# A graph network's edge loop: nine instead of eight blocks per pair of turns fetched by TensorE, and a reordered prologue

## The reference

```python
def _gatv2_layer(x, src, dst, Wl, Wr, a, b):
    xl = (x @ Wl).reshape(N, H, O)
    xr = (x @ Wr).reshape(N, H, O)
    s = jax.nn.leaky_relu(xl[src] + xr[dst], NEG_SLOPE)
    e = jnp.einsum('eho,ho->eh', s, a)
    m = jax.ops.segment_max(e, dst, num_segments=N)
    ex = jnp.exp(e - m[dst])
    denom = jax.ops.segment_sum(ex, dst, num_segments=N)
    alpha = ex / (denom[dst] + 1e-16)
    out = jax.ops.segment_sum(xl[src] * alpha[:, :, None], dst, num_segments=N)
    return out.reshape(N, H * O) + b
# GIN: agg = segment_sum(relu(x[src] + edge_attr @ W_edge.T + b_edge), dst), then linear, batch norm, relu, linear
```

## Time and profile before

| what | value |
|---|---|
| time, median of 3 runs | 6675.94 us (6675.53 to 6676.13) |
| the profiled execution | 6672.46 us, span of its core 6670.6 us |
| busy: PE, PEld, DVE, ACT, POOL | 82%, 66%, 74%, 69%, 73% |
| DMA | 1096.16 MB, 164 GB/s over the span |

### The profile page before, as it was taken

How to read it: one execution, slowest core, us unless ns; L and a number is a source line. 1 busy time by engine, 2 the same in 40 slices (tenths; PEclk the granted TensorE clock), 3 DMA queues, 4 the chain that set the end, 5 groups by cost and what they waited for, 6 DMA issues and landing times.

```text
span 6670.6 us, 91041 instructions
## 1 busy us (share of the span) xinstructions
PE 5440.5 (82%) x23034; PEld 4434.7 (66%) x23034; DVE 4960.0 (74%) x7160; ACT 4603.5 (69%) x6121; POOL 4896.3 (73%) x5107
## 2 busy tenths in 40 slices
PE   2588888888668888888848888888875999999996
PEld 1476777777457777777736777777764777777774
DVE  7599999999659888888847888888885444333333
ACT  1487877877458888888827888888873555555553
POOL 3777777777677777777767777777767777777774
PEclk9999999999779999999959999999997999999997
DMA  9466666666435555555524555555542444444441
GB/s 377 174 218 216 217 219 217 218 217 215 131 117 163 162 162 163 165 164 166 164 75 147 166 165 165 165 163 162 162 152 82 132 132 136 134 132 132 132 134 57
DMA packets 420529, 1096.16 MB, mean 164 GB/s; under 512 B 162288, under 2 KB 183424, under 8 KB 416278
## 3 DMA queue, kind: packets, MB, share of 16 engines
q1 hardware_dynamic: 242306, 863.40, 35.7%
q0 software_dynamic: 164080, 181.10, 13.0%
q10 hardware_dynamic: 14116, 51.39, 2.0%
HBM read 710.56 MB, written 384.88 MB: 164 GB/s over the span
## 4 chain that ended last, share of the span: by engine, by line
POOL 47%; issue 26%; DVE 14%; ACT 7%; DMA 2%; PE 2%; ACTq 1%; DVEq 0%; POOLq 0%; SPq 0%
POOL sb_xl L512 42%; DVE pG L1137 4%; ACT sb_turn_out L705 3%; POOL sb_hot_f L512 3%; DVE sb_s_run L1179 3%; ACT sb_hot L705 3%; POOL marks L516 2%; DVE sb_s L1412 2%; DMA sb_xl<-xl_table,sb_idx 1%; PE pG L593 1%; DVE sb_mark L1083 1%; DVE sb_e_in L1201 1%; DVE sb_lr L1199 1%; DVE sb_s L1197 1%; ACT pB L705 1%
## 5 line engine op out<-in xcount | busy, mean ns | idle before, releaser
L593 PE MATMUL pG<-sb_xl_parts,sb_hot 128*128 128x476 f32 (+1 forms) x21952 | 5059.9, 389 | 860.4 <-ACT sb_xl L705 618.0
L512 POOL DMA_INDIRECT sb_xl<-xl_table,sb_idx x4704 | 4502.7, 957 | 1450.0 <-issue 1429.0
L593 PEld LDWEIGHTS pG<-sb_xl_parts,sb_hot 128*128 128x128 f32 x21952 | 4222.5, 195 | 1740.5 <-issue 1180.0
L1137 DVE COPY_PREDICATED pG<-sb_pick_turn,pG 128x408 f32<-128x408 int32 (+5 forms) x2352 | 1008.9, 431 | 932.4 <-ACT sb_pick_turn L705 809.2
L705 ACT ACTIVATE sb_hot<-sb_wide 128x1792 fp32r<-128x1792 bf16 x784 | 1316.8, 1693 | 76.7 <-ACT sb_turn_out L705 71.4
L1179 DVE TENSOR_TENSOR_SCAN sb_s_run<-pB,sb_v_in 128x272 f32<-128x272 f32 (+2 forms) x1075 | 1084.4, 1017 | 25.2 <-ACT sb_turn_out L705 4.0
L705 ACT ACTIVATE sb_turn_out<-sb_s_run 128x1088 f32<-128x1088 f32 (+3 forms) x395 | 833.5, 2110 | 10.5 <-DVE sb_s_run L1179 10.3
L705 ACT ACTIVATE sb_xl<-pG 128x136 f32<-128x136 f32 (+3 forms) x826 | 241.2, 294 | 711.2 <-DVE pG L1137 589.5
L1176 DVE TENSOR_TENSOR_SCAN pB<-sb_same_c,pB 128x1024 f32<-128x1024 f32 x294 | 672.1, 2286 | 0.1
L705 ACT ACTIVATE sb_v_in<-sb_v_g 128x1024 f32<-128x1024 f32 x291 | 597.1, 2052 | 0.0
L705 ACT ACTIVATE pB<-sb_mark 128x960 f32<-128x960 f32 x294 | 551.8, 1877 | 11.8 <-DMA sb_mark<-marks 1.4
(11 more groups left out here) (235 smaller groups left out, 2372.8 us busy)
## 6 DMA issues: line engine op xcount, KB each, us to landing
sb_wide<-hots SPq DMA_DIRECT2D x294, 896.0 KB
state_rows<-sb_turn_out SPq DMA_DIRECT2D x294, 576.0 KB
sb_mark<-marks SPq DMA_DIRECT2D x294, 512.0 KB
sb_wide<-codes SPq DMA_DIRECT2D x98, 896.0 KB
hots<-sb_wide SPq DMA_DIRECT2D x98, 896.0 KB, 3.7
sb_xl<-xl_table,sb_idx POOLq DMA_INDIRECT x4704
marks<-sb_hot_f SPq DMA_DIRECT2D x32, 1568.0 KB
agg_rows<-sb_turn_out ACTq DMA_DIRECT2D x98, 512.0 KB
```

What stands on the lines that cost most here:

```text
L512: return pool.indirect_dma_start(out=dst, out_offset=None, in_=table, in_offset=bass.IndirectOffsetOnAxis(ap=index, axis=0))
L593: product = pe.matmul(pG[:, a, 0:GB * n], hot[k][:, m, a * P:(a + 1) * P], rows[:, :, 0:n], start=(m == 0 and part == 0), stop=(m == GB - ...
L1137: return dve.copy_predicated(rows[:, :, 0:n], over(pick_turn[:, k, stage, lo:hi], n), rows[:, :, at:at + n])
```

## The change

It does five things.

1. In the three attention layers the second turn of each pair fetches five blocks by TensorE and eleven by GpSimd; the first stays at four and twelve. The extra block makes the first share of that turn three blocks. `pG` grows from four to five PSUM banks, `pB` shrinks from four to three. The GIN layer keeps four and twelve.
2. To fit, the factor tile `f` in PSUM shrinks from 9 to 5 outputs of 4 heads (612 to 340 values), and the sum scans become four of 20, 16, 16 and 16 channels.
3. ACT computes `neg_h` as Identity with scale and bias from `same`; the tile `neg` and its DVE instruction go.
4. At the start of a layer the first turn's widening, products, selection and copy no longer stand behind `xr_first`.
5. Prologue: the fill is issued after 14 loads, in one loop; six loads of late weights and `w_blk` go behind it; the splitters' round trip moves to ACT's queue; the ranks are shifted by one matmul and a DVE copy.

```diff
+FETCHED = (4, 5)
+PAIR = sum(FETCHED)
+MOST = max(FETCHED)
+SHARES = tuple(((0, n - 2), (n - 2, n)) for n in FETCHED)
+SHARE_BANK = (0, MOST - 2)
+GD = tuple(G - n for n in FETCHED)
+FO = 5
+SUMS = (0, FO * 4, 36, 52, 68)
...
-        pG = ctx.enter_context(nc.psum_tensor("pG", [P, 4, 512], F32))
+        pG = ctx.enter_context(nc.psum_tensor("pG", [P, MOST, 512], F32))
...
             sp.dma_start(pe_src_r, t["src_pe_edges"]).then_inc(s_src, 16)
+            sp.wait_ge(s_zero, 1)
+            with sp.Fori(0, J * C // (B * C)) as i:
+                sp.dma_start(marks_runs[:, bass.ds(i * (B * C), B * C)], zeros[:, 0:B * C]).then_inc(s_filled, 16)
+            sp.dma_start(b_all[:, :], t["b_rows"].partition_broadcast(P)).then_inc(s_late, 16)
...
-            sp.wait_ge(s_rank, 1)
-            sp.dma_start(ranks[1:1 + NB].rearrange("(p b) -> p b", p=P), ranks_i[:, 0, :]).then_inc(s_rank_out, 16)
-            sp.wait_ge(s_rank_out, 32)
-            sp.dma_start(ranks_i[:, 1, :], ranks[0:NB].rearrange("(p b) -> p b", p=P)).then_inc(s_rank_in, 16)
...
+            def code_row(turn, k):
+                sp.dma_start(staged_code[k].rearrange("p (m e) -> p m e", m=GB),
+                             codes[bass.ds(turn, 1), :].rearrange("a (m e) -> (a m) e", m=GB)[:, ECX - EC[k]:ECX].partition_broadcast(P)
+                             ).then_inc(s_code[k], 16)
...
-                        turn_gathers(l * PAIRS + i, k, range(GD))
+                        turn_gathers(l * PAIRS + i, k, range(GD[k]))
...
+                    pe.wait_ge(s_rank, 1)
+                    pe.matmul(pB[:, 512:513], next_lane[:, :], ranks_f[:, 0, B - 1:B], start=True, stop=True).then_inc(s_rank, 1)
...
+            act.dma_start(splitters.rearrange("(p k) -> p k", p=P), split_s[:, :]).then_inc(s_split_out, 16)
+            act.wait_ge(s_split_out, 16)
+            act.dma_start(split_all, splitters.partition_broadcast(P)).then_inc(s_split_in, 16)
...
-                copy(neg_h[:, :, :], neg[:, bass.ds(turn, 1), :].to_broadcast([P, H, G1])).then_inc(s_e_carried, 1)
+                act.activation(neg_h[:, :, :], same[:, bass.ds(turn, 1), :].to_broadcast([P, H, G1]), ACT.Identity, bias=neg_col[:, 0:1], scale=-NEG).then_inc(s_e_carried, 1)
...
-                return act.activation(f_half[:, :, :, 1:G1], wf_arg[:, 1].unsqueeze(1).to_broadcast([P, HALF, H, G]), ACT.Exp)
+                return act.activation(f_part[:, :, :, 1:G1], wf_arg[:, 1].unsqueeze(1).to_broadcast([P, FO, H, G]), ACT.Exp)
...
-                act.wait_ge(s_start, l + 1)
...
                     rows_copied(l * TURNS + 1, l * PAIRS, q, 0)
+                act.wait_ge(s_start, l + 1)
+                act.sem_inc(s_passed, 1)
+                turn_marks((l * PAIRS + 1) * 16, 0)
...
+                for q in range(2):
+                    select_rows(l * TURNS + 1, l * TURNS + 1, l * (2 * TURNS) + q, 0, q)
                 dve.wait_ge(s_xr_first, (l + 1) * 16)
...
-                    scan_sums(f_flat, 0, HALF * H)
+                    scan_sums(f_flat, SUMS[0], SUMS[1])
                     select_stage(1 - k, 1, 1).then_inc(s_pick, 1)
                     dve.wait_ge(s_pick, picks + 4)
-                    scan_sums(f_flat, HALF * H, HALF * H + third)
+                    scan_sums(f_flat, SUMS[1], SUMS[2])
                     select_stage(1 - k, 1, 2).then_inc(s_sel[1], 1)
-                    scan_sums(f_flat, HALF * H + third, V).then_inc(s_sums, 1)
+                    scan_sums(f_flat, SUMS[2], SUMS[3])
+                    scan_sums(f_flat, SUMS[3], SUMS[4]).then_inc(s_sums, 1)
```

More of the change, by code:

```diff
@@ L52 @@
 GROUPS = B // GB
-EC = GE * P
-HOT = GB * EC
+EC = tuple(n * P for n in FETCHED)
+HOT = tuple(GB * n for n in EC)
+ECX, HOTX = max(EC), max(HOT)
 PARTS = 2
@@ L58 @@
 HO = O + 1
-HALF = HO // 2 + 1
+FO = 5
+SUMS = (0, FO * 4, 36, 52, 68)
+LIN_SUMS = (0, 22, 43, 64)
 V = H * HO
@@ L126, in build @@
         at = PARTS * B * TW
[L127 to L130, removed]
+        staged, staged_code = [], []
+        for k in range(2):
+            codes_k = wide[:, at:at + HOT[k] // 2]
+            staged.append(codes_k.bitcast(BF16).rearrange("p (m e) -> p m e", m=GB))
+            staged_code.append(codes_k.bitcast(I16))
+            at += HOT[k] // 2
         left = wide[:, at:at + GB * TW]
@@ L420, in load_code @@
                 sp.sem_inc(s_passed, 1)
-                sp.dma_start(staged_code[k], codes[bass.ds(turn, 1), :].rearrange("a e -> (a e)").partition_broadcast(P)
-                             ).then_inc(s_code[k], 16)
+                code_row(turn, k)
             def tables_out(l):
@@ L562, in _, with share @@
                     gather(node_rows[:, b, 0:C], agg_rows, last_edge[:, b:b + 1]).then_inc(s_nrow[g], 16)
+        def share(k, q, n=TW):
+            shares, banks = (LIN_SHARES, LIN_SHARE_BANK) if n == C else (SHARES, SHARE_BANK)
+            lo, hi = shares[k][q]
+            return lo, hi, banks[q]
         def place(psum, i):
@@ L588, in pe_gather @@
                     pe.sem_inc(s_passed, 1)
-                for a in range(*SHARES[q]):
+                lo, hi, bank = share(k, q, n)
+                for a in range(lo, hi):
                     for m in range(GB):
@@ L592, in pe_gather @@
                             rows = xl_part[part][:, m * GB * TW:(m + 1) * GB * TW].rearrange("p (b c) -> p b c", b=GB)
-                            product = pe.matmul(pG[:, a, 0:GB * n], hot[k][:, m, a * P:(a + 1) * P], rows[:, :, 0:n],
+                            product = pe.matmul(pG[:, bank + a - lo, 0:GB * n], hot[k][:, m, a * P:(a + 1) * P], rows[:, :, 0:n],
                                                 start=(m == 0 and part == 0), stop=(m == GB - 1 and part == PARTS - 1))
@@ L630, in attention_layer @@
                     for k in range(2):
-                        for q in range(len(SHARES)):
+                        for q in range(2):
                             pe.wait_ge(s_wide[q], l * TURNS + 2 * i + (k + 1))
@@ L743, in widen, with widen_both @@
                 act.sem_inc(s_passed, 1)
-                lo, hi = SHARES[q]
+                lo, hi, bank = share(k, q, n)
                 copy(hot[k][:, :, lo * P:hi * P], staged[k][:, :, lo * P:hi * P]).then_inc(s_wide[q], 1)
-            def widen_both(ready, filled, used, k):
-                for q in range(len(SHARES)):
-                    widen(ready, filled, used, k, q)
+            def widen_both(ready, filled, used, k, n=TW):
+                for q in range(2):
+                    widen(ready, filled, used, k, q, n)
             def widen_first(l, i, k, fresh):
@@ L923, in linear_turn @@
                 act.wait_ge(s_sums, turn_all)
-                copy(same_half.rearrange("p (c g) -> p c g", g=G1), same[:, bass.ds(turn, 1), :].to_broadcast([P, C // 2, G1]))
+                copy(same_part.rearrange("p (c g) -> p c g", g=G1), same[:, bass.ds(turn, 1), :].to_broadcast([P, LIN_SUMS[1], G1]))
                 copy(v_lin[:, :, 0:1], lin_run[:, :, G:G1]).then_inc(s_same, 1)
@@ L1193, in attention_turn @@
                 dve.wait_ge(s_xr, turn_all + 1)
-                for q in range(len(SHARES)):
+                for q in range(2):
                     dve.wait_ge(s_rows[q], turn_all + 1)
-                dve.wait_ge(s_xl[k], (use + 1) * (16 * GD))
+                dve.wait_ge(s_xl[k], (use + 1) * (16 * GD[k]))
                 tt(s[:], xl[:, k, :, 0:C], xr.rearrange("p c g -> p g c"), ALU.add).then_inc(s_added, 1)
@@ L1267, in attention_layer @@
                 scan_xr(l * TURNS)
-                for q in range(len(SHARES)):
-                    select_rows(l * TURNS + 1, l * TURNS + 1, l * (2 * TURNS) + q, 0, q)
                 if build:
```

189 lines of the change are left out of this document (92 added, 97 removed).

## The result

The changed kernel takes 6513.83 us (median of 4 runs, 6513.23 to 6514.41), the kernel before 6675.81 (6675.53 to 6676.13). The ratio is 0.9759, 95% interval 0.9746 to 0.9771: 2.4% faster. The profiled executions lie 158.05 us apart (6672.46 and 6514.41), the medians 162.0. Predicted were 155.3 between the profiled executions, and a median of 6521 us in a range of 6502 to 6590. Two slow executions are left out of all ratios: one of the run with a gather left out (14054 us) and one of the kernel before beside the last four runs (9217 us).

A forecast was written before the change was run, and what follows sets the result against it. GpSimd issuing gathers was taken as the bound. Layers two and three 124.4, first layer 21 and prologue 9.9 us sum to 155.3, from 6672.46 to 6517.2 profiled, 6521 us as median; range 6502 to 6590.

The forecast's parts named there:

- The extra block in layers two and three: Second and third attention layers: 23 gathers per pair instead of 24, GpSimd still the bound, each layer saving 61.3 us.
- The scan in four pieces, the wider copies: DVE in layers two and three: copies +0.43 and scans +0.14 us per pair, making its pair 28.51 us.
- TensorE: Attention layers: 126 products take 27.96 us per pair, under GpSimd's 28.78, leaving 0.8 us; clock stays at its upper level.
- The rival at 6590: TensorE takes over in layers two and three: a remaining clock drop makes its pair 29.5 us, +69 us; chance 0.16.
- ACT: Attention turns: widening at most +0.85 us per pair, smaller factor copy saves some; 25.3 of 28.8 us, hidden by idle time.
- the slower rival: ACT reloads tables each turn for Identity in `neg_h`, two loads of 1283 ns; 6800 us; chance 0.07 with anything else slower.
- GpSimd's waits at the layers' start: Layers two and three: waits of 2.39 and 1.25 us for the first turn go, where 0.30 is usual; +3.0 us gained.
- First layer: First attention layer: DVE becomes the bound at 30.78 us per pair, 14 us gained, plus 7 from the earlier start; 21 together.
- Prologue: Before the layers: no ranks' round trip and an earlier fill let the scatters start 9.9 us earlier.
- GIN layer: Layer after the attention layers: claimed not changed in what sets its pace; no term in the sum.

The follow-up runs named there:

- the last four runs: Changed kernel with five blocks in each pair's first turn instead of its second, with and without the late first turn, each twice; ratios 0.977, 0.9775, 0.9785, 0.9788.
- the dose of eight products: Changed kernel with four more TensorE products, sums overwritten, at the start of each attention turn's first share, eight per pair; ratio 0.9907, scaled 6613.7 us.

## Why the prediction was right

- **The extra block in layers two and three**: 61.3 us each by gathers, measured 58.6 with the late start (1616.82 before, 1558.25 with the first turn late). Right. In the third layer it is 58.1. GpSimd stayed the bound by 0.36 us per pair, where 28.78 less 28.51 had given 0.27; DVE's pair is 28.36.
- **The scan in four pieces, the wider copies**: the copy of 612 values took 0.80 us, the 340-value scan 0.865. DVE's pair of 28.51 was 0.15 too long.
- **TensorE**: 27.96 us per pair and 0.8 of slack; the dose of eight products measured 27.94 and 0.78. The share of 42 products took 9.32 us and 98 in a row 21.82, no 7.46 us is left among the steady shares of layers two and three, and the clock is 1.00 there (0.98 in the first layer, where TensorE still waits up to 2.4 us). The rival at 6590 needed one of the clock's drops to stay. The idle time that stood ahead of the slow share, 2.69 us in the earlier trace rows, is gone there: the longest wait is 0.7.
- **ACT**: the widening of 2688 values took 2.44 us (at most 2.54 was allowed), the factor copy 0.42 instead of 0.64. The copy for `neg_h` with scale and bias is 0.34 us, and there are still three table loads in the whole trace, of 1283 ns each. So the slower rival had no base. (Its price was summed a little high as well: 32.4 less 31.07 is 1.33 us, not 1.4.) The Trainium skill ("ScalarE: Activation LUTs", "Table sets: the hidden batching unit") says that cheap functions such as identity are in every table set. The trace agrees: an Identity between exponentials brought no load.
- **GpSimd's waits at the layers' start**: +3.0 us over both layers, but the early start is worth 6.0 + 5.5 in the changed kernel. This is the term that was sized wrong. I took only the waits that the kernel before showed and called them gone. That the extra block itself would lengthen them, by the gather less and by the larger share in front of the multiplication, I did not see. It did no harm, since the change moves the first turn too. With eight blocks the same early start returns nothing (1616.79 us against 1616.82).
- **First layer**: 14 us from the pair and 7 from the earlier start, 21 together; measured 18.7 and 4.6, 23.3. From the first turn's start to the last's, DVE's pair came out at (1727.42 - 5.3 - 239.48) / 48.5 = 30.57 us instead of 30.78. But the kernel before took 30.95 by the same marks, not the 31.07 of the window, so that two errors of 0.21 and 0.12 in part cancel: 0.38 per pair instead of 0.29. GpSimd's pair was put at 29.77 by keeping the mean of a gather; the long gathers come with the builds, two per pair whatever the number of gathers, and the run with a gather left out gives 30.15. That changed nothing, since DVE's is longer. The start gave less because the twelve gathers didn't land 2.3 us after their issue: the first went out at 219.81, the turn began 19.7 us later instead of 17.3. The DMA engines, nearly idle when the first turn began before the change (0.14 between 245 and 253), were full, with loads of codes and a store of one-hot matrices among the work:

```profile
225.00:234.00 9.00, 0.00 (x0) 0.00 (x0) 2.59 (x2) 1.33 (x3) 6.87 (x8) 0.50 0.88 321
234.00:240.00 6.00, 0.00 (x0) 0.00 (x0) 1.67 (x2) 2.37 (x2) 4.78 (x5) 0.50 0.95 366
```

  That this held up the landings is read from these rows, and no run tested it.

- **Prologue**: 9.9 us, measured 9.55. The experiments show that it rests on both edits. The end of the fill near 157, read from the DMA share, was not the end of the wait for it: with the fill late and the ranks known early the scatter went out at 160.03.
- **GIN layer**: called unchanged; it took 2.4 us longer (160.8 to 158.4). The run with eight blocks shows the same layer time within 0.6 us, so it isn't the ninth block's. The GIN layer has edits of its own, which the prediction passed over: with the smaller `pB` its sums are scanned in three pieces (357, 357 and 374 values) where the kernel before has two of 544. No run puts them back, and the cause stays open.

Sum of the measured terms: 9.4 + 23.3 + 64.6 + 63.6 - 2.4 = 158.5, against 158.05 between the profiled executions and 9.9 + 21 + 124.4 = 155.3 predicted. That the sum is only 3 us off is partly luck: layers two and three gave 3.8 us more than said and the first 2.3, and the GIN layer took 2.4 back. The forecast of the median missed by 7 us, of which 4.1 are the offset: it was put 3.5 us above the profiled execution, as before, and lies 0.6 below.

## What to carry to other kernels

When the bound engine issues equal things back to back, one of them less is worth its full period only up to the second engine's distance; find that by a pair's busy and wait time, not by the busy share of the span. A step that costs nothing in the steady state can still cost at the start of every loop, where the lead between engines isn't built up yet: count which buffer the bound engine needs first and what stands in front of the instruction that frees it. Two edits that each shorten a different road to the same start are to be made together: here each alone gave 3.5 or 4.4 us, both 9.55.

## What the runs showed of the hardware

- TensorE's clock at a layer's start. After the products of the first turn it stands still until the second turn's may begin, at a granted clock of 0.50 in the first layer (the rows above). The next 28 products took 8.61 us, where a steady share of 28 takes 6.28:

```profile
248.28 8.61 PE L604 MATMUL pG<-sb_xl_parts,sb_hot 128*128 128x476 f32 x28 [40.53 <-ACT sb_xl L719]
```

  In layers two and three it is 9.06 us after 25.59 of idle and 7.87 after 25.17.
- A GpSimd gather keeps its period of 1.249 to 1.252 us (a body of 0.944 to 0.948 and a pause of 0.30) in layers two and three, with 112, 126 or 134 products per pair beside it, as long as it doesn't wait for DVE; in no run did it go faster. Beside a one-hot build of DVE's, in the first layer, its body was 1.72 us in the mean.
- In the four runs with five blocks first TensorE's work was broken by pauses that no instruction explains, more than once per pair. The timeline of the third layer in one of them, start and duration:

```profile
3498.78 3.19 PE L604 MATMUL pG<-sb_xl_parts,sb_hot 128*128 128x476 f32 x14
3509.74 17.25 PE L604 MATMUL pG<-sb_xl_parts,sb_hot 128*128 128x476 f32 x70 [7.77 <-remote]
```

The row of waits from 3000 to 4200, a stretch of 62 turns, counts 38 of them, 248.0 us in 1200:

```profile
PE pG L604 <- remote: 248.0, 38, 7.8
```

No semaphore of this kernel is named as their releaser, the gathers keep 945 ns and DVE's scan of `xr` its 2.29 us; only TensorE stands, and its granted clock in this stretch is 0.89. The kernel before was just as slow beside them (9016 and 9086 us), so it isn't the edit. What holds TensorE there no run shows.
